# Two fused FFN layers with a top-2 router: routing by VectorE's block transposes, and T1's sums from GpSimd to VectorE

## The reference

```python
def layer(x, W0, b0, A, Bw, scale, W1, b1, W_router, lora_A, lora_B):      # per batch: A, Bw chosen by id
    y = x @ W0.T + b0 + scale * (x @ A.T) @ Bw.T
    probs = softmax(y @ W_router.T)                     # 8 experts
    p, i = top_k(probs, 2); p = p / sum(p)
    w = sum(one_hot(i, 8) * p[..., None], axis=1)       # token x expert
    h = einsum('td,erd->ter', y, lora_A)                # rank 16
    return x + y @ W1.T + b1 + 2.0 * einsum('ter,eor,te->to', h, lora_B, w)
```

## Time and profile before

| | us |
|---|---|
| median of 3 runs | 686.79 |
| lowest, highest | 685.77, 687.58 |
| the profiled execution, its own time | 686.49 |
| its span, first to last instruction | 684.8 |
| TensorE busy | 678.8 |
| VectorE busy | 423.3 |
| GpSimd busy | 261.6 |
| ScalarE busy | 231.6 |

### The profile page before, as it was taken

One profiled execution on the slowest core, in us unless ns is written; L12 is line 12 of the kernel. 1 busy time (PEld: TensorE's weight loads), 2 busy tenths in 40 slices (PEclk: granted clock), 3 DMA queues, 4 the chain that ended last, 5 costly groups with the idle time before them and its releaser, 6 DMA issues.

```text
span 684.8 us, 9215 instructions
## 1 busy us (share of the span) xinstructions
PE 678.8 (99%) x3299; PEld 598.0 (87%) x3299; DVE 423.3 (62%) x719; ACT 231.6 (34%) x429; POOL 261.6 (38%) x217
## 2 busy tenths in 40 slices
PE   8999999999999999999999999999999999999997
PEld 7999999888888888888899999998888888888886
DVE  5664667868855474862673753788698437738423
ACT  6444244645221034220514344266352302422200
POOL 2373023036583150395134433030647625105930
PEclk9999999999999999999999999999999999999999
DMA  8345756993768944547742755689846886535633
GB/s 291 115 156 185 262 196 205 392 386 130 245 194 327 326 123 124 157 145 254 276 176 72 235 167 182 246 279 371 333 127 212 282 342 196 181 116 168 199 106 123
DMA packets 74132, 147.25 MB, mean 215 GB/s; under 512 B 6948, under 2 KB 38308, under 8 KB 73958
## 3 DMA queue, kind: packets, MB, share of 16 engines
q1 hardware_dynamic: 70678, 138.20, 58.7%
q10 hardware_dynamic: 1872, 6.36, 2.9%
q0 software_dynamic: 1536, 2.10, 1.1%
HBM read 98.42 MB, written 47.33 MB: 213 GB/s over the span
## 4 chain that ended last, share of the span: by engine, by line
PE 97%; DMA 1%; SPq 1%; ACT 0%; DVE 0%; issue 0%
PE ps L605 45%; PE ps L489 15%; PE ps L490 15%; PE ps L491 15%; PE ps L564 4%; PE ps L621 2%; DMA e_raw<-in_ext 1%; PE ps L614 1%; SPq L289 0%; PE ps L587 0%; ACT e_hl L715 0%; SPq L266 0%; DVE w_hl L977 0%; DVE w L1186 0%; ACT w_hl L724 0%
## 5 line engine op out<-in xcount | busy, mean ns | idle before, releaser
L605 PE MATMUL ps<-x_hl,a_hl 128*128 128x512 f32 x1344 | 317.8, 394 | 0.0
L605 PEld LDWEIGHTS ps<-x_hl,a_hl 128*128 128x128 f32 x1344 | 251.3, 188 | 53.3 <-issue 0.3
L489 PE MATMUL ps<-e_hl,w_hl 128*128 128x384 f32 (+1 forms) x432 | 146.2, 338 | 0.8 <-DVE e_hl L977 0.7
L490 PE MATMUL ps<-e_hl,w_hl 128*128 128x384 f32 (+1 forms) x432 | 145.8, 337 | 0.0
L491 PE MATMUL ps<-e_hl,w_hl 128*128 128x384 f32 (+1 forms) x432 | 145.5, 337 | 0.0
L489 PEld LDWEIGHTS ps<-e_hl,w_hl 128*128 128x128 f32 x432 | 81.3, 188 | 2.7 <-issue 1.3
L490 PEld LDWEIGHTS ps<-e_hl,w_hl 128*128 128x128 f32 x432 | 81.3, 188 | 0.0
L491 PEld LDWEIGHTS ps<-e_hl,w_hl 128*128 128x128 f32 x432 | 81.3, 188 | 0.0
L977 DVE TENSOR_TENSOR x_hl<-x_raw,x_hl 128x512 fp32r<-128x512 f32 x64 | 60.8, 1004 | 8.4 <-ACT x_hl L811 8.4
L1363 POOL TENSOR_TENSOR w<-x_raw 128x512 f32<-128x512 f32 x16 | 23.8, 1515 | 103.8 <-DMA x_raw<-in_xT 32.7
L977 DVE TENSOR_TENSOR w_hl<-w_raw,w_hl 128x1024 fp32r<-128x1024 f32 (+2 forms) x24 | 20.6, 868 | 58.0 <-ACT w_hl L702 51.1
(11 more groups left out here) (118 smaller groups left out, 896.9 us busy)
## 6 DMA issues: line engine op xcount, KB each, us to landing
a_hl<-form_scratch SPq DMA_DIRECT2D x112, 512.0 KB, 5.0
...
```

Source lines behind the costliest of these rows:

```text
L489: nc.tensor.matmul(dst, w_hi, m_hi, start=start, stop=False, skip_group_check=again)
L490: nc.tensor.matmul(dst, w_hi, m_lo, start=False, stop=False, skip_group_check=again)
L605: last = nc.tensor.matmul(ps[:, bank, :], a_hl[:, n % NM, k, w, :], x_hl[:, slot, k, x, :], start=start and i == 0, stop=i == 3 * KH - 1, ...
```

## The change

- Logits: one matmul per half in `inner_low`, with the router's columns repeated 16 times as weights (`rt_cols`, copied by ScalarE in `router_cols`), gives the 8 logits of 512 tokens in every group of 8 partitions. The four small logit matmuls, the four transposes and ScalarE's copy of h go.
- `routing` transposes these logits in 32x32 blocks on VectorE, finds best and second best by reductions and comparisons over 16 groups of 8, and makes for each partition only the two experts it needs (`WANT`); it spreads them to 512 columns and transposes them back into `hg`. `gated` reads h from PSUM.
- T1's sums are made by VectorE (`make_t1`), not by GpSimd. GpSimd makes T4's sums first and `add_12` behind them.
- In the second half VectorE does all of T1's and T3's low parts ahead of `routing`, then `gated` and the first `keep_u2`, then hg's low part. TensorE does both first W3 tiles ahead of their `low_and_experts`.
- In the next lists, instructions on places in SBUF are named by them: `low_mv_86` is `low_mv` of the second half, `u_60`, `w_61`, `c_62` are `u2`, `w57`, `c21`.

The diff, cut to its core:

```diff
-        gates = place("gates", [P, TT, ER], f32, at[0] - CH * 4)
-        h_sb = place("h_sb", [P, CH], f32)
+        by_token = place("by_token", [P, GR, SQ], f32)
+        rt_cols = place("rt_cols", [P, P], f32r, at[0] - CH * 4)
...
+        lg, lg2 = (by_token[:, :, i * NE:(i + 1) * NE] for i in range(2))
+        top = [place(f"top{i}", [P, GR, 1], f32) for i in range(2)]
+        first_of = [place(f"first_of{i}", [P, GR, 1], f32) for i in range(2)]
+        gap = place("gap", [P, GR, 1], f32)
+        ex = place("ex", [P, GR, 1], f32)
+        den = place("den", [P, GR, 1], f32)
+        wa, wb = first_of
...
-                    pe.wait_ge(S["gate_done"], u)
+                    pe.wait_ge(S["logit_read"], u)
...
+                pe.wait_ge(S["rt_done"], u + 1)
+                nc.tensor.matmul(ps[:, S_BANK, :], rt_cols[:], low_mv[tb][:], start=True,
+                                 stop=True).then_inc(S["pe_logit"], 1)
...
-                if gates_of is not None:
-                    pe.wait_ge(S["h_done"], 2 * g + gates_of + 1)
-                    pe.wait_ge(S["gate_done"], 2 * g + gates_of + 1)
...
-                    if logits_of is not None and i < TT:
-                        tb = logits_of
-                        logit = nc.tensor.matmul(ps[:, S_BANK, i * NE:(i + 1) * NE], low_mv[tb][:, i * P:(i + 1) * P],
-                                                 stack[tb][:, D + ER:EXT], start=True, stop=True)
-                        if i == TT - 1:
-                            logit.then_inc(S["pe_logit"], 1)
-                    if gates_of is not None and i < TT:
-                        gate = nc.tensor.transpose(ps[:, H_BANK, i * P:(i + 1) * P], gates[:, i, :], ident_sb[:])
-                        if i == TT - 1:
-                            gate.then_inc(S["pe_gate"], 1)
...
-                            if m == 0:
-                                pe.wait_ge(S["hg_lo"], 2 * g + 2)
-                            low_and_experts(0, 1, m, BANK_C12[m])
+                            if m >= 2:
+                                low_and_experts(0, 1, m, BANK_C12[m])
...
+            def router_cols(l, g, tb):
+                u = 2 * g + tb
+                if tb:
+                    act.wait_ge(d_stack[1], 48 * (g + 1))
+                elif g % SUPER:
+                    act.wait_ge(d_stack[0], 48 * (l + 1))
+                else:
+                    act.wait_ge(S["stack_in"], l + 1)
+                act.wait_ge(S["eye_done"], 2)
+                act.wait_ge(S["pads_done"], 3)
+                if u:
+                    act.wait_ge(S["hg_done"], u)
+                nc.scalar.copy(rt_cols[:].rearrange("p (n e) -> p n e", e=NE),
+                               stack[tb][:, D + ER:EXT].bitcast(f32).unsqueeze(1).broadcast_to([P, P // NE, NE])
+                               ).then_inc(S["rt_done"], 1)
...
-            def inner(g, tb):
-                act.wait_ge(S["pe_h"], 2 * g + tb + 1)
-                if g + tb:
-                    act.wait_ge(S["hg_done"], 2 * g + tb)
-                nc.scalar.copy(h_sb[:], ps[:, H_BANK, :]).then_inc(S["h_done"], 1)
...
-                    t1_split(g, range(2))
-                    inner(g, 1)
-                    t1_split(g, range(2, 3))
+                    router_cols(l, g, 1)
+                    t1_split(g)
                     top_exp(g, 1)
-                    t1_split(g, range(3, 4))
                     keep_w5(g, 0)
                     hg_split(g, 1)
                     keep_w5(g, 1)
...
+            def make_t1(g):
+                dve.wait_ge(S["pe_hx"], 2 * g + 2)
+                for k in range(KH):
+                    dve.wait_ge(S["t2_done"], KH * g + k + 1)
+                    sub(x_sum[:, SLOT_OF[g % SUPER][T1], k, 1, :], raw_of(B22, k), c21[:, k, :]
+                        ).then_inc(S["t1_done"], 1)
...
                 dve.wait_ge(S["pe_logit"], u + 1)
-                chain(nc.vector.tensor_tensor(lg[:], ps[:, S_BANK, 0:TT * NE].rearrange("p (t e) -> p t e", t=TT),
-                                              bias_r[:].unsqueeze(1).broadcast_to([P, TT, NE]), ALU.add))
-                nc.vector.memset(gap[:], 0.0)
-                for t in range(TT):
-                    ins = nc.vector.max(top[:, t, :], lg[:, t, :])
-                chain(ins)
-                sub(gap[:], top[:, :, 1:2], top[:, :, 0:1]).then_inc(S["gap_done"], 1)
-                for t in range(TT):
-                    ins = nc.vector.max_index(top_i[:, t, :], top[:, t, :], lg[:, t, :])
-                chain(ins)
-                chain(nc.vector.tensor_copy(top_f[:], top_i[:]))
-                chain(nc.vector.tensor_tensor(ma[:], iota_sb[:], top_f[:, :, 0:1].broadcast_to([P, TT, NE]),
-                                              ALU.is_equal), False)
-                chain(nc.vector.tensor_tensor(mb[:], iota_sb[:], top_f[:, :, 1:2].broadcast_to([P, TT, NE]),
-                                              ALU.is_equal), False)
+                ins = nc.vector.transpose(by_token[:].rearrange("p g c -> p (g c)"), ps[:, S_BANK, :])
+                ins.then_inc(S["logit_read"], 1)
+                dve.wait_ge(S["logit_read"], u + 1)
+                chain(nc.vector.tensor_tensor(lg, lg,
+                                              bias_r[:].unsqueeze(1).broadcast_to([P, GR, NE]), ALU.add))
+                for i, (v, m, gate) in enumerate(((lg, ma, ga), (lg2, mb, gb))):
+                    chain(nc.vector.tensor_reduce(top[i][:], v, AXIS.X, ALU.max))
+                    chain(nc.vector.tensor_tensor(m[:], v, over(top[i], NE), ALU.is_equal))
+                    if i:
+                        sub(gap[:], top[1][:], top[0][:]).then_inc(S["gap_done"], 1)
+                    chain(nc.vector.tensor_tensor(m[:], m[:], ranks, ALU.mult))
+                    chain(nc.vector.tensor_reduce(first_of[i][:], m[:], AXIS.X, ALU.max))
+                    if i == 0:
+                        chain(nc.vector.tensor_tensor(m[:], over(first_of[i], NE), ranks, ALU.is_equal))
+                        chain(nc.vector.scalar_tensor_tensor(lg2, m[:], -3.0e38, lg, op0=ALU.mult, op1=ALU.add), False)
+                    chain(nc.vector.tensor_tensor(gate[:], over(first_of[i], WANT), wanted, ALU.is_equal))
                 dve.wait_ge(S["exp_done"], u + 1)
                 chain(nc.vector.tensor_scalar(den[:], ex[:], 1.0, None, ALU.add))
                 chain(nc.vector.reciprocal(wb[:], den[:]))
                 chain(nc.vector.tensor_scalar(wa[:], wb[:], 2.0, None, ALU.mult))
-                chain(nc.vector.tensor_tensor(den[:], ex[:], wa[:], ALU.mult))
-                chain(nc.vector.tensor_tensor(ma[:], ma[:], wa[:].broadcast_to([P, TT, NE]), ALU.mult), False)
-                chain(nc.vector.tensor_tensor(mb[:], mb[:], den[:].broadcast_to([P, TT, NE]), ALU.mult))
-                nc.vector.tensor_tensor(gates[:].rearrange("p t (e r) -> p (t e) r", r=R),
-                                        *(m[:].rearrange("p t e -> p (t e)").unsqueeze(2)
-                                          .broadcast_to([P, TT * NE, R]) for m in (ma, mb)),
-                                        ALU.add).then_inc(S["gate_done"], 1)
+                chain(nc.vector.tensor_tensor(den[:], ex[:], wa[:], ALU.mult), False)
+                chain(nc.vector.tensor_tensor(ga[:], ga[:], over(wa, WANT), ALU.mult))
+                chain(nc.vector.tensor_tensor(gb[:], gb[:], over(den, WANT), ALU.mult))
+                chain(nc.vector.tensor_tensor(by_token[:].rearrange("p g (n r) -> p g n r", r=R),
+                                              *(m[:].unsqueeze(3).broadcast_to([P, GR, WANT, R]) for m in (ga, gb)),
+                                              ALU.add))
+                chain(nc.vector.transpose(hg[:], by_token[:].rearrange("p g c -> p (g c)")))
             def gated(g, tb):
                 u = 2 * g + tb
-                dve.wait_ge(S["h_done"], u + 1)
-                dve.wait_ge(S["pe_gate"], u + 1)
-                nc.vector.scalar_tensor_tensor(hg[:], h_sb[:], bias_sb[:, KT:KT + 1], ps[:, H_BANK, :],
+                dve.wait_ge(S["pe_h"], u + 1)
+                nc.vector.scalar_tensor_tensor(hg[:], ps[:, H_BANK, :], bias_sb[:, KT:KT + 1], hg[:],
                                                op0=ALU.add, op1=ALU.mult).then_inc(S["hg_done"], 1)
-                dve.wait_ge(S["hg_hi"], u + 1)
+            def gated_low(g, tb):
+                dve.wait_ge(S["hg_hi"], 2 * g + tb + 1)
                 sub(hg_hl[:, tb, 1, :], hg[:], hg_hl[:, tb, 0, :].bitcast(f32)).then_inc(S["hg_lo"], 1)
...
-                    made_split(g, T1, range(2))
+                    made_split(g, T1)
+                    sum_split(g, T3, w57)
                     routing(g, 1)
-                    made_split(g, T1, range(2, 4))
-                    sum_split(g, T3, w57)
-                    for m in range(KH):
+                    gated(g, 1)
+                    keep_u2(g, 0)
+                    gated_low(g, 1)
```

(11 more changed lines are left out.)

67 lines of the change are left out of this document (39 added, 28 removed).

## The result

| | before | after |
|---|---|---|
| median (6 runs each) | 686.50 | 695.29 |
| lowest, highest | 685.77, 687.58 | 693.12, 696.72 |
| the profiled execution | 686.49 | 694.96 |
| its span | 684.8 | 693.3 |

The ratio is 1.0125, with a 95% interval of 1.0112 to 1.0138: slower by 8.8 us, where the forecast was 6.2. The granted clock is 0.993 over the profiled span. Of the six executions the one with clock 1.000 has a span of 691.4, and the one with 0.990 has 695.0; the forecast's span was 691.0.

What follows compares the result with a forecast made beforehand. TensorE, busy 678.8 of 684.8 us, was taken to bound the kernel. 5.7 us won on small matmuls and 11.9 lost in waits gave +6.2, so 693.0 us against a median of 686.79; range 681.2 to 698.0.

Steps and rivals of the forecast that it cites:

- The small matmuls, -5.7: TensorE, each of 8 halves: eight small matmuls (0.94 us) go, one full logit matmul (0.23) comes; 5.7 us less.
- The routing's length, 8.1 free: VectorE's routing: 8.1 us from its start until hg is made, when no GpSimd sum disturbs it.
- Its start: VectorE, second half: routing begins behind T1's and T3's low parts, at 176.1 in pair 0 and 286.5 in pair 1.
- The collision, 3.5 and 3.6: Second half: VectorE operations with two SBUF inputs wait out GpSimd's T4 sums; routing loses 3.5 us (pair 0), 3.6 (pair 1).
- slips through: Rival, chance 0.22: the routing's small operations pass between GpSimd's reads, loss under 1 us; 681.4 to 683 us.
- half of it: Rival, chance 0.10: two routing operations pass per GpSimd sum, loss about 2 us; no change, 686.8 us.
- Who waits: TensorE at second-half W3 products, for ScalarE's second W5 copy behind hg's high part; pair 0's 3.6 us in two pieces.
- The four losses, 3.6, 2.3, 3.7, 2.3: TensorE's waits in us in the second halves of pairs 0 to 3, from the collision; 11.9 in all.
- The clock: Rival, chance 0.08: TensorE's clock falls in the four new waits, 2.1 us each, +8.4 on the forecast: 701.4 us.
- T1 on VectorE costs nothing: Second half: T1 would be ready at 284.1 in pair 1, W5 wants it at 289.1; moving its sums costs nothing.
- Nothing is late behind it: Behind hg: U2's additions end about 4 us later, but W7's last tile needing them is 10 us on; no wait.
- the faster case: The rival where short routing operations pass GpSimd's sums, chance 0.22, 681.4 to 683 us; the range was drawn to reach it.

Runs made afterwards that it cites:

- run 1: Changed kernel, but GpSimd's T4 sums also wait until hg of the second half is made: 681.29 us, ratio 0.9932 to the kernel before.
- run 11: Changed kernel with T4's sums waiting for hg, plus eight small 8-column matmuls more in each half of a pair (64 in all): 687.32 us.
- run 2: Changed kernel, but only the third and fourth of T4's sums wait for hg: 686.86 us, ratio 1.0010 to the kernel before.
- run 12: Changed kernel plus eight unused 512-column matmuls (1.8 us) ahead of W3's first tile in each second half: 694.89 us.
- run 9: Changed kernel with T4's sums waiting for hg and T1's sums given back to GpSimd: 681.98 us, ratio 0.9935 to the kernel before.
- run 5: Changed kernel with GpSimd making U2's additions first and T4's sums behind them, as before the change: 693.34 us, ratio 1.0094.
- run 6: Changed kernel with T4's sums behind U2's additions and ScalarE's T4 high parts behind the last two W5 copies: 691.54 us.

## Why the prediction was right, and where it was off

From the second half's logit matmul to the first expert tile TensorE needs 19.49 us when nothing is late (as in pairs 1 and 3 of run 1). The changed kernel took 23.50, 21.86, 23.60 and 23.43: 4.0, 2.4, 4.1 and 3.9 lost.

- *The small matmuls, -5.7:* right, by the 34.91 against 35.63 us a half and by run 11.
- *The routing's length, 8.1 free:* 8.20. The trace of before had no such transpose or reduction; scaled by size they were put at 0.68 and 0.27, and they took 0.71 and 0.29.
- *Its start:* 176.1 and 176.21 in pair 0. In pair 1 the forecast had 286.5, and 288.54 less the 1.9 us by which the pair began later is 286.6.
- *The collision, 3.5 and 3.6:* 3.7 and 3.4, one operation for each sum. In pair 1 the first three that wait are the three that were forecast; the fourth is the second gate mask (0.84), while the product with the ranks passes. The forecast counted two gaps of before that had waited for a GpSimd sum; there were three (0.63, 0.63 and 0.62 us), which only adds to its reason. Runs 1 and 2 show the collision to be the cause: without it 681.3, with half of it 686.9. The rivals "slips through" and "half of it" are out as forecasts of the changed kernel, but each is the right time of the version in which that much of the collision is left.
- *Who waits:* right for pairs 1 and 3, TensorE at W3's second tile for the W5 copy behind hg's high part. In pairs 0 and 2 the forecast had two pieces, 2 us ahead of the first tile and 1.6 ahead of the second. The first came (1.90 and 1.91); of the second 0 and 0.18 were left, as the clock had slowed the tile between. With the clock up, in run 12, it is there (1.52).
- *The four losses, 3.6, 2.3, 3.7, 2.3:* mis-sized in pair 3 (3.9), and 0.4 short in 0 and 2, where run 1 shows some 0.5 us of short waits even without the collision.
- *The clock:* the rival had it right that it falls, and its price of 2.1 behind each wait was wrong: 1.6 in pair 3, none in pair 1, and in pairs 0 and 2 it only took the place of the second wait. My reason against it, that the wait comes in two pieces, did not hold: the clock fell behind pieces of 1.90 us. TensorE: Matmul & The Clock Gate of the Trainium skill (Why this matters for your kernels) advises against idle gaps, but against longer ones than these; here the clock fell behind 1.90, 1.91 and 2.03 us and not behind another 2.03, and the measurement decides.
- *T1 on VectorE costs nothing:* right (run 9).
- *Nothing is late behind it:* right for the changed kernel, and narrow: runs 5 and 6, with T4 behind the additions, had waits of up to 2.7 us.

Sum: -5.7 + 14.4 = 8.7, and the spans differ by 8.5. By the rows, the 2.3 us between the forecast and the median are pair 3's clock (1.6) and the 0.4 in each of pairs 0 and 2. An execution of the changed kernel with clock 1.000 had a span of 691.4 against the forecast's 691.0. Run 12 does not bear this out for the whole time, since its spans at full clock are 692.4 to 694.1, so the clock's share of the 2.3 us is argued and not shown. That the collision makes the loss is shown, by runs 1 and 2. The forecast's range, 681.2 to 698.0, reached from the faster case to the slowest but one, so the measured time alone would say little for the working; the rows do.
